# Products without a result on TensorE, ahead of and inside the first attention of an eight-block transformer kernel

## The chip, the cores and the metric

The kernel runs on one core of a Trainium2 chip. The metric is the device time of one execution in microseconds (us), as the median of several runs. Five engines with queues of their own matter here: TensorE (PE in the profile, with PEld for its weight loads), VectorE (DVE), ScalarE (ACT), GpSimd (POOL) and SyncE (SP, which issues the transfers). Each engine runs its instructions in order, and the engines wait for one another by semaphores.

## The reference, cut to what matters

The input x is 2 sequences of 512 tokens with 512 features. Eight blocks follow one another, each of the form x + f(layernorm(x)). The change lies in the first one, an attention with small latents:

```python
C_q  = x @ Wq_d + bq_d            # 512 -> 12
C_kv = x @ Wkv_d + bkv_d          # 512 -> 4
q = (C_q @ W_qk + b_qk).reshape(b, s, 32, 4)
scores = einsum('bqhd,bkd->bhqk', q, C_kv) / sqrt(4)
attn = softmax(scores, -1)
V = (C_kv @ Wv_u + bv_u).reshape(b, s, 32, 16)
out = einsum('bhqk,bkhd->bqhd', attn, V).reshape(b, s, 512)
return out @ Wo + bo
```

The seven blocks behind it (feed-forward with adapters, two larger attentions, a smaller one and two routed feed-forwards) are untouched.

## The kernel before

`attn0a_block` computes the first attention. It has two parts.

**The opening.** The 1024 tokens are 8 tiles of 128. For each tile t, VectorE takes the mean and variance (`norm.statistics`, L90 and L92) and forms factors (L100, L102), ScalarE takes the root (L96) and normalises the tile (`norm.normalise`, L109), TensorE turns it with four 128x128 transposes (`norm.turn`, L118), and ScalarE and VectorE copy the turned tile out of PSUM as a high and a low part (L123, L127). The tiles arrive by one DMA each. Between tiles 5, 6 and 7 TensorE starts on the latent projection (`latents`, three products for each block of 128 features, L37 to L39), and finishes it behind tile 7 in one stream: parts 0 to 3 of `latents`, with the first queries (`project_queries(0)`) between them.

**The steps.** 16 steps, each for 4 groups of heads and one sequence, run in a software pipeline over `step` and `g` (8 values of g in a step). In the step's own turn, `scores(step, g)` (L1584) writes scores by query into one of two PSUM tiles, and VectorE takes maxima over them (`maximum`, L1467). One call of `scores` is issued an iteration ahead: iteration g issues the scores of g + 1. When the maxima of a step are there, TensorE turns them (`turn_maxima`, L1569) and VectorE forms the shifted queries (`shift`, L1473, behind the first maximum of the next step in its queue). One step later TensorE computes the scores again by key (`scores_by_key`, L1596, two PSUM tiles `by_key`), ScalarE takes their exponentials (L1364), and TensorE multiplies by the values (`times_v`, L1618). In this stage, three bf16 products of zeros by the mask constant (`add_zeros`, L1608) add nothing to `out`; they stand in iterations 3, 5, 7 and 1 from step 1 on. Step 0 has only `scores`, `turn_values` (L1535) in its first two iterations, and `project_queries(1)` in iteration 1; on ScalarE it has nothing but the values' copy and one signed copy of queries.

`zeros` is a 128x128 bf16 tile that GpSimd fills at the start (L1312, semaphore `s_zeros`). `m.ident16` and `m.mask` are bf16 constants that arrive by DMA (semaphore `s_const`). Two later attentions have products of the same kind: eight of them at L2326 in `attn0b_block` and five at L3471 in `attn1b_block`, all of 256 columns of the mask constant by the bf16 identity.

Of the kernel before, what the change touches and what calls it, by code (L numbers as in the profile page):

```python
# [25 lines left out]
P = 128  # L26
# [1167 lines left out]
def attn0a_block(nc, m, d, prefix):  # L1194
# [19 lines left out]
    fills = [("Q", 0)]  # L1214
# [10 lines left out]
    with ExitStack() as ctx:  # L1225
# [24 lines left out]
        zeros, s_zeros = n.sb("zeros", [P, P], BF16), n.sem("zeros")  # L1250
        by_query = [n.ps(f"by_query{i}", [P, 2, SEQ]) for i in range(2)]
        by_key = [n.ps(f"by_key{i}", [P, SEQ]) for i in range(2)]
        aux, out = n.ps("aux", [P, QT, P]), n.ps("out", [P, QT, P])
# [16 lines left out]
        s_pv, s_osb, s_recip, s_out = [n.sem(k) for k in ("pv", "osb", "recip", "tokens")]  # L1270
        block = ctx.enter_context(nc.Block(no_gpsimd_drain=True))
        LOADS = 4
        aux_flat = aux[:, :, :].rearrange("p t q -> p (t q)")

        @block.sync
# [44 lines left out]
        def _(act):  # L1320
            act.wait_ge(s_eps, 1)
            norm.root(act, m, 0)
            for t in range(TILES + 1):
# [6 lines left out]
                if t == 3:  # L1330
                    act.wait_ge(s_load, 16 * LOADS)
                    act.activation(down_hi[:, :, :], down[:, :, :], ACT.Copy).then_inc(s_hi, 1)
# [186 lines left out]
        def _(pe):  # L1519
            def latents(g, parts=range(KT)):  # L1520
                pe.wait_ge(norm.s_lo, QT * (g // 2 + 1))
                if g >= 2:
                    pe.wait_ge(s_latev, g - 1)
                for k in parts:
                    last = mm3(pe, proj[g % 2], pair(down_hi, down_lo, slice(None), k, bass.ts(g % 2, P)),
                               pair(m.xnT_hi, m.xnT_lo, slice(None), k, bass.ts(g // 2, SEQ)),
                               start=k == 0, stop=k == KT - 1)
                    if k == KT - 1:
                        last.then_inc(s_lat, 1)

            def turn_values(b):

                pe.wait_ge(s_latev, 2 * (b + 1))
                for at in range(QT):
                    last = pe.transpose(out[:, b, bass.ts(at, VW)], lat[VROWS, 1, bass.ts(b * QT + at, P)],  # L1535
                                        m.ident[VROWS, VROWS])
                last.then_inc(s_vps, 1)

            def merge(k):

                last = pe.matmul(by_query[0][bass.ts(k, VW), 0, :], wv[:, k, :], wo[:, k, :], start=True, stop=True)
                if k == KT - 1:
                    last.then_inc(s_merged, 1)

            def merge_bias(k):
                if k == 0:
                    pe.wait_ge(s_wo, 48)
                last = pe.matmul(by_query[1][:, 0, :], bv[:, k, :], wo[:, k, :], start=k == 0, stop=k == KT - 1)
                if k == KT - 1:
                    last.then_inc(s_bias_v, 1)  # L1550
# [7 lines left out]
            def project_queries(step):  # L1558
                turn, b = divmod(step, BATCH)
                pe.wait_ge(s_lo, 3 + min(step, 1))  # L1560
                aux_free(("Q", step))
                mm3(pe, aux_flat, pair(wqk_hi, wqk_lo, slice(None), bass.ts(turn, P)),
                    pair(lat_hi, lat_lo, slice(0, QLAT + 1), bass.ts(b, SEQ)), start=True, stop=True).then_inc(s_aux, 1)

            def turn_maxima(step):
                pe.wait_ge(s_max, NG * (step + 1))
                aux_free(("M", step))
                for qt in range(QT):
                    last = pe.transpose(aux[:, qt, :], negmax[:, step % 2, qt, :], m.ident[:, :])  # L1569
                last.then_inc(s_aux, 1)  # L1570

            def scores(step, g):
                qt, a = g // 2, 1 - g % 2
                b = step % BATCH
                if NG * step + g >= 2:
                    pe.wait_ge(s_max, NG * step + g - 1)
                if g == 0:
                    pe.wait_ge(s_q, step + 1)
                    pe.wait_ge(s_kmix, 1 + min(step, 1))
                if step == 0 and g < 2:  # L1580
                    pe.wait_ge(s_latev, 3 + g)
                for e in range(2):
                    rows = slice(GROUP * (2 * a + e), GROUP * (2 * a + e + 1))
                    last = pe.matmul(by_query[g % 2][:, e, :], queries[rows, step % 2, bass.ts(qt, P)],  # L1584
                                     keys[rows, bass.ts(b, SEQ)], start=True, stop=True)
                last.then_inc(s_by_query, 1)

            def scores_by_key(step, u):
                kt, j = divmod(u, G)
                b = step % BATCH  # L1590
                if NU * step + u >= 2:
                    pe.wait_ge(s_exp, NU * step + u - 1)
                if u == 0:
                    pe.wait_ge(s_shifted, step + 1)
                rows = slice(GROUP * j, GROUP * (j + 1))
                pe.matmul(by_key[u % 2][:, :], keys[rows, bass.ts(b * QT + kt, P)], shifted[rows, step % 2, :],  # L1596
                          start=True, stop=True).then_inc(s_by_key, 1)
# [14 lines left out]
            def times_v(step, kt):  # L1612
                turn, b = divmod(step, BATCH)
                pe.wait_ge(s_exp, NU * step + G * (kt + 1))
                if kt == 0 and step >= 1:
                    pe.wait_ge(s_osb, step)
                for j in range(G):
                    last = pe.matmul(out[VW * j:VW * (j + 1), :, :].rearrange("v t q -> v (t q)"),  # L1618
                                     values[:, b * QT + kt, :],
                                     probsT[step % 2][:, kt, j, :, :].rearrange("p t q -> p (t q)"),  # L1620
                                     start=kt == 0, stop=kt == QT - 1)
                last.then_inc(s_pv, 1)

            def back_to_tokens(step):
                pe.wait_ge(s_osb, step + 1)
                aux_free(("T", step))
                for qt in range(QT):
                    last = pe.transpose(aux[:, qt, :], o_sb[:, step % 2, qt, :], m.ident[:, :])
                last.then_inc(s_aux, 1)

            pe.wait_ge(s_ident, 16)
            for t in range(TILES):
                norm.turn(pe, m, t)
                if t == 5:
                    pe.wait_ge(s_lo, 1)
                    latents(0, range(0, 1))
                if t == 6:
                    latents(0, range(1, 2))
# [3 lines left out]
            project_queries(0)  # L1642
            latents(3)
            pe.wait_ge(s_ones, 1)
            pe.wait_ge(s_zeros, 1)
            pe.wait_ge(s_const, 32)
            scores(0, 0)
            for step in range(STEPS + 2):
                for g in range(NG):
                    if g == 0 and step >= 2:  # L1650
                        scores_by_key(step - 2, NU - 2)
                        scores_by_key(step - 2, NU - 1)
                    if g >= 1 and 1 <= step <= STEPS:
                        scores_by_key(step - 1, 2 * g - 2)
                        scores_by_key(step - 1, 2 * g - 1)
                    after = NG * step + g + 1
                    if after < NG * STEPS:
                        scores(after // NG, after % NG)
                    if g == 0 and 1 <= step <= STEPS:
                        turn_maxima(step - 1)  # L1660
                    if g in (0, 2) and step >= 2:
                        times_v(step - 2, 2 + g // 2)
                    if g in (4, 6) and 1 <= step <= STEPS:
                        times_v(step - 1, (g - 4) // 2)
                    if g == 1 and step + 1 < STEPS:
                        project_queries(step + 1)
                    if step == 0 and g < BATCH:
                        turn_values(g)
                    if step == STEPS and 1 <= g <= 2:
                        merge_bias(2 * g - 2)  # L1670
                        merge_bias(2 * g - 1)
                    if step == STEPS and 3 <= g <= 4:
                        merge(2 * g - 6)
                        merge(2 * g - 5)
                    if g == 3 and 1 <= step <= STEPS:
                        add_zeros(first=step - 1)
                    if g in (5, 7) and 1 <= step <= STEPS or g == 1 and step >= 2:
                        add_zeros()
                    if g == 5 and step >= 2:
                        back_to_tokens(step - 2)  # L1680
# [2013 lines left out]
```

## Time and profile before

| | |
|---|---|
| median of 3 runs | 2195.97 us (2193.91 to 2198.79) |
| the profiled execution's own time | 2193.78 us |
| its span, first to last instruction | 2192.1 us |
| TensorE busy | 2046.3 us, 93% of the span |
| mean granted TensorE clock | 0.974 of full speed |

The durations in the next section come from the one profiled execution. The difference between its own time and its span, 1.68 us, lies around the first and last instruction. The granted clock of a stretch is 1.00 at the 2.4 GHz level and 0.50 at the 1.2 GHz level.

### The profile page before, as it was taken

What the parts mean: (1) busy time and instruction counts of PE and PEld (TensorE: products, weight loads), DVE (VectorE), ACT (ScalarE), POOL (GpSimd) and SP (SyncE); (2) the same over time, 40 slices, a digit from 0 to 9 for tenths busy, and PEclk for the clock granted to TensorE, in tenths of its full rate; (3) what the DMA queues carried; (4) which work ended last, traced back from release to release, by engine and by line L of the source; (5) the groups of instructions that cost most, each with busy time, mean ns of one, the idle gap of its engine ahead of it and who ended that gap; (6) DMA issues with size and microseconds to landing.
All of it is one profiled execution on the core that took longest, in us unless ns stands there. A gap on an engine that the chain in (4) does not pass through costs nothing. (4 is left out here: it accounts for less than half of the span.)

```text
span 2192.1 us, 33417 instructions
## 1 busy us (share of the span) xinstructions
PE 2046.3 (93%) x11617; PEld 1467.6 (67%) x11617; DVE 1391.3 (63%) x2509; ACT 1164.6 (53%) x2691; POOL 832.0 (38%) x1011
## 2 busy tenths in 40 slices
PE   6999988999999999999998789999999987999988
PEld 4333356777888888888876667777777765844457
DVE  6888574546666666666655646666666556777756
ACT  5777553245655656566554555555555534345553
POOL 0000100145545545455340145545554421747611
PEclk8999989999999999999999999999999999999999
DMA  3000022761112021121111344344333220744301
GB/s 121 1 1 1 3 97 81 222 197 39 48 40 67 22 68 39 49 68 39 30 39 51 93 111 114 91 105 116 91 92 73 61 73 30 215 89 73 73 25 39
DMA packets 95733, 158.10 MB, mean 72 GB/s; under 512 B 12064, under 2 KB 33568, under 8 KB 93391
## 3 DMA queue, kind: packets, MB, share of 16 engines
q1 hardware_dynamic: 85774, 134.19, 21.6%
q0 software_dynamic: 9792, 21.77, 4.2%
q8 instruction: 95, 1.56, 0.3%
q14 instruction: 72, 0.58, 0.1%
HBM read 90.91 MB, written 31.46 MB: 56 GB/s over the span
## 5 line engine op out<-in xcount | busy, mean ns | idle before, releaser
L2576 POOL TENSOR_TENSOR attn1a_probs<-attn1a_probs,attn1a_recip 128x128 f32<-128x128 f32 (+3 forms) x256 | 179.1, 721 | 231.8 <-DVE attn1a_recip L2759 231.2
L1917 POOL TENSOR_TENSOR attn0b_probs<-attn0b_probs,attn0b_recip 128x128 f32<-128x128 f32 (+3 forms) x256 | 196.6, 790 | 184.0 <-DVE attn0b_recip L2161 184.0
L2630 ACT ACTIVATE attn1a_probs<-attn1a_scores,attn1a_negmax 128x128 f32<-128x128 f32 (+3 forms) x256 | 132.9, 525 | 172.8 <-DVE attn1a_negmax L2745 171.6
L2021 ACT ACTIVATE attn0b_probs<-attn0b_scores,attn0b_negmax 128x128 f32<-128x128 f32 (+3 forms) x256 | 133.0, 525 | 121.4 <-DVE attn0b_negmax L2154 120.9
L1467 DVE TENSOR_REDUCE attn0a_negmax<-attn0a_by_query 128x2 f32<-128x1024 f32 x128 | 151.9, 1219 | 10.2 <-PE attn0a_by_query L1584 10.2
L2745 DVE TENSOR_REDUCE attn1a_negmax<-attn1a_scores 128x2 f32<-128x256 f32 (+3 forms) x128 | 105.4, 824 | 68.8 <-PE attn1a_scores L2950 68.8
L1910 POOL TENSOR_TENSOR attn0b_q_cos<-attn0b_q_cos,attn0b_q_swap 128x512 f32<-128x512 f32 x64 | 84.4, 1318 | 159.2 <-DVE attn0b_q_swap L2143 159.2
L2029 ACT ACTIVATE attn0b_probsT_hi<-attn0b_turned 128x256 fp32r<-128x256 f32 (+3 forms) x128 | 90.2, 704 | 87.4 <-PE attn0b_turned L2305 85.8
L2154 DVE TENSOR_REDUCE attn0b_negmax<-attn0b_scores 128x2 f32<-128x256 f32 (+3 forms) x128 | 105.0, 820 | 45.8 <-PE attn0b_scores L2294 45.8
L2962 PE MATMUL attn1a_turned<-ident_f,attn1a_probs 128*128 128x128 f32 x640 | 116.0, 279 | 8.8 <-DVE attn1a_probsT L2753 7.4
L2140 DVE TENSOR_TENSOR attn0b_q_cos<-attn0b_aux,attn0b_cos_q 128x512 f32<-128x512 f32 x60 | 41.5, 692 | 115.9 <-ACT attn0b_q_swap L2042 115.9
L2962 PEld LDWEIGHTS attn1a_turned<-ident_f,attn1a_probs 128*128 128x128 f32 x640 | 75.8, 141 | 50.6 <-POOL attn1a_probs L2576 19.8
L2166 DVE TENSOR_TENSOR attn0b_probsT_lo<-attn0b_turned,attn0b_probsT_hi 128x256 fp32r<-128x256 f32 (+3 forms) x128 | 104.4, 816 | 5.0 <-ACT attn0b_probsT_hi L2029 4.3
L1317 POOL TENSOR_TENSOR x_resident<-x_resident,attn0a_out_bias 128x512 f32<-128x512 f32 x8 | 9.9, 1281 | 256.3 <-DVE attn0a_out_bias L1489 256.3
L37 PE MATMUL attn0b_aux<-xnT,attn0b_wq_hi 128*128 128x512 f32 x240 | 99.6, 415 | 4.6 <-DVE x_resident L2176 2.4
L2305 PE MATMUL attn0b_turned<-ident_f,attn0b_probs 128*128 128x128 f32 x640 | 91.3, 273 | 10.4 <-DVE attn0b_probsT_lo L2166 10.4
L37 PE MATMUL attn0b_aux<-attn0b_wo_hi,attn0b_oT_hi 128*128 128x512 f32 x256 | 100.0, 391 | 0.9 <-DVE x_resident L2176 0.9
L2042 ACT ACTIVATE attn0b_q_swap<-attn0b_aux 64x512 f32<-64x512 f32 x120 | 71.2, 593 | 55.4 <-PE attn0b_aux L39 53.2
L39 PE MATMUL attn0b_aux<-attn0b_wo_lo,attn0b_oT_hi 128*128 128x512 f32 x256 | 100.1, 391 | 0.0
L38 PE MATMUL attn0b_aux<-attn0b_wo_hi,attn0b_oT_lo 128*128 128x512 f32 x256 | 99.6, 389 | 0.0
L2305 PEld LDWEIGHTS attn0b_turned<-ident_f,attn0b_probs 128*128 128x128 f32 x640 | 77.2, 141 | 29.0 <-DVE attn0b_probsT_lo L2166 12.7
L2946 PE MATMUL attn1a_scores<-xnT,attn1a_qT 128*128 128x128 f32 (+3 forms) x256 | 92.2, 360 | 3.3 <-DMA attn1a_qT<-attn1a_stage 3.3
(543 smaller groups left out, 6187.5 us busy)
## 6 DMA issues: line engine op xcount, KB each, us to landing
pre<-in_b_o SPq DMA_DIRECT2D x16, 1024.0 KB, 5.6
attn1a_qT<-attn1a_stage SPq DMA_DIRECT2D x128, 128.0 KB, 3.2
attn1a_qT<-attn1a_stage SPq DMA_DIRECT2D x64, 256.0 KB, 3.9
attn0b_vals<-attn0b_v_out SPq DMA_DIRECT2D x16, 512.0 KB, 3.7
attn0b_keys<-attn0b_part SPq DMA_DIRECT2D x32, 256.0 KB, 4.2
pre<-in_b_q SPq DMA_DIRECT2D x8, 1024.0 KB, 7.6
attn0b_kT<-attn0b_keys SPq DMA_DIRECT2D x64, 128.0 KB, 2.8
pre<-in_b_kv SPq DMA_DIRECT2D x5, 1024.0 KB, 6.8
```

The source lines that it names most:

```text
L37: pe.matmul(out, lhs[0], rhs[0], start=start, stop=False)
L39: return pe.matmul(out, lhs[0], rhs[1], start=False, stop=stop)
L1467: dve.tensor_reduce(into, by_query[g % 2][:, :, :], AX.X, ALU.max, negate=True).then_inc(s_max, 1)
L1917: pool.tensor_tensor(x, x, recip[:, r % DEEP, e:e + 1].broadcast_to([P, (qt + 1) * P]), ALU.mult).then_inc(s_scaled, 1)
L2021: act.activation(probs[:, r % DEEP, e, 0:width], scores[r % 2][:, e, 0:width], ACT.Exp, bias=negmax[:, r % 2, e:e + 1], accum_out=sums[:, ...
L2154: dve.tensor_reduce(negmax[:, r % 2, :], scores[r % 2][:, :, 0:(qt + 1) * P], AX.X, ALU.max, negate=True).then_inc(s_max, 1)
L2166: dve.tensor_tensor(of_pair(probsT_lo, at, qt, p), turned[:, :, 0:qt + 1, :], of_pair(probsT_hi, at, qt, p).bitcast(F32), ALU.subtract).th ...
L2305: last = pe.transpose(turned[:, e, k, :], probs[:, r % DEEP, e, bass.ts(k, P)], m.ident[:, :])
L2576: pool.tensor_tensor(x, x, recip[:, r % DEEP, e:e + 1].broadcast_to([P, (qt + 1) * P]), ALU.mult).then_inc(s_scaled, 1)
L2630: act.activation(probs[:, r % DEEP, e, 0:width], scores[r % 2][:, e, 0:width], ACT.Exp, bias=negmax[:, r % 2, e:e + 1], accum_out=sums[:, ...
L2745: dve.tensor_reduce(negmax[:, r % 2, :], scores[r % 2][:, :, 0:(qt + 1) * P], AX.X, ALU.max, negate=True).then_inc(s_max, 1)
L2962: last = pe.transpose(turned[:, k, :], probs[:, r % DEEP, e, bass.ts(k, P)], m.ident[:, :])
```

## The change

Three groups of products are added to TensorE's queue, none with a result that anything reads, and one wait moves.

- `WARM_START`: 48 products of zeros by zeros (128 columns each) ahead of the wait for the identity and the first tile. The wait for `s_zeros`, which stood ahead of the first scores, moves in front of them.
- `WARM`: 14 such products behind the transposes of each of tiles 0 to 4.
- `FILLS`: in step 0, in each iteration g from 1 to 7, five bf16 products of 256 columns of the mask constant by the bf16 identity, behind the scores. They write the first `by_key` tile, which nothing uses before step 1.

```diff
+        WARM_START, WARM, FILLS = 48, (14, 14, 14, 14, 14), 5
...
+            def warm_up(fills):
+
+                for _ in range(fills):
+                    pe.matmul(out[:, 0, :], zeros[:, :], zeros[:, :], start=True, stop=True)
+
+            pe.wait_ge(s_zeros, 1)
+            warm_up(WARM_START)
             pe.wait_ge(s_ident, 16)
             for t in range(TILES):
                 norm.turn(pe, m, t)
+                if t < len(WARM):
+                    warm_up(WARM[t])
                 if t == 5:
                     pe.wait_ge(s_lo, 1)
                     latents(0, range(0, 1))
...
             pe.wait_ge(s_ones, 1)
-            pe.wait_ge(s_zeros, 1)
             pe.wait_ge(s_const, 32)
             scores(0, 0)
...
                     if step == 0 and g < BATCH:
                         turn_values(g)
+                    if step == 0 and g >= 1:
+                        for _ in range(FILLS):
+                            pe.matmul(by_key[0][:, 0:2 * P], m.ident16[:, :],
+                                      m.mask[:, :, :].rearrange("p e x -> p (e x)"), start=True, stop=True)
```

## Rows read from the trace of the kernel before

**Rows 1.** Windows: length, busy PE, PEld, DVE, ACT, POOL; clock; DMA share, GB/s
```profile
39.35:47.37 8.02, 5.54 (x16) 2.17 (x16) 7.22 (x7) 0.23 (x1) 0.00 (x0) 0.50 0.52 195
47.37:56.20 8.83, 7.89 (x34) 3.43 (x34) 7.21 (x7) 4.81 (x9) 0.00 (x0) 0.50 0.00 1
61.89:75.40 13.51, 12.70 (x91) 5.15 (x95) 11.18 (x13) 9.65 (x19) 0.00 (x0) 1.00 0.00 1
1921.00:1927.00 6.00, 6.00 (x51) 3.92 (x49) 5.58 (x6) 0.00 (x0) 0.02 (x1) 1.00 1.42 198
1930.00:1933.80 3.80, 3.58 (x21) 1.75 (x20) 3.03 (x3) 2.97 (x7) 0.64 (x1) 0.99 0.00 0
1933.90:1937.00 3.10, 3.10 (x18) 1.13 (x16) 1.23 (x1) 0.69 (x2) 0.64 (x1) 0.50 0.00 0
```

**Rows 2.** Timeline of the opening: start, duration, instruction, idle before it and releaser
```profile
0.84 0.21 POOL L1312 MEMSET attn0a_zeros<- 128x128 bf16 x1
8.12 2.09 PE L118 MATMUL attn0a_by_query<-ident_f,attn0a_o_sb 128*128 128x128 f32 x8 [8.12 <-ACT attn0a_o_sb L109]
11.83 1.12 PE L118 MATMUL attn0a_by_query<-ident_f,attn0a_o_sb 128*128 128x128 f32 x4 [1.63 <-ACT attn0a_o_sb L109]
...
18.12 1.12 PE L118 MATMUL attn0a_by_query<-ident_f,attn0a_o_sb 128*128 128x128 f32 x4 [1.20 <-ACT attn0a_o_sb L109]
...
21.17 0.81 ACT L109 ACTIVATE attn0a_o_sb<-x_resident,attn0a_norm_offset,attn0a_norm_rstd 128x512 f32<-128x512 f32 x1 [0.69 <-DVE attn0a_norm_offset L102]
...
22.36 0.60 PE L118 MATMUL attn0a_by_query<-ident_f,attn0a_o_sb 128*128 128x128 f32 x4
```

**Rows 3.** Timeline of VectorE in steps 0 and 1
```profile
40.84 5.74 DVE L1467 TENSOR_REDUCE attn0a_negmax<-attn0a_by_query 128x2 f32<-128x1024 f32 x5
47.37 0.69 DVE L1473 TENSOR_TENSOR attn0a_shifted<-attn0a_aux,attn0a_queries 128x512 fp32r<-128x512 f32 x1 [0.80 <-PE attn0a_aux L1569]
50.95 1.23 DVE L1467 TENSOR_REDUCE attn0a_negmax<-attn0a_by_query 128x2 f32<-128x1024 f32 x1 [0.63 <-PE attn0a_by_query L1584]
...
56.62 1.23 DVE L1467 TENSOR_REDUCE attn0a_negmax<-attn0a_by_query 128x2 f32<-128x1024 f32 x1 [1.40 <-PE attn0a_by_query L1584]
58.25 1.23 DVE L1467 TENSOR_REDUCE attn0a_negmax<-attn0a_by_query 128x2 f32<-128x1024 f32 x1 [0.41 <-PE attn0a_by_query L1584]
59.70 1.23 DVE L1467 TENSOR_REDUCE attn0a_negmax<-attn0a_by_query 128x2 f32<-128x1024 f32 x1 [0.23 <-PE attn0a_by_query L1584]
61.89 0.69 DVE L1473 TENSOR_TENSOR attn0a_shifted<-attn0a_aux,attn0a_queries 128x512 fp32r<-128x512 f32 x1 [0.96 <-PE attn0a_aux L1569]
```

**Rows 4.** Timeline of TensorE in step 0 and the turn of its maxima
```profile
45.50 0.79 PE L1584 MATMUL attn0a_by_query<-attn0a_keys,attn0a_queries 32*128 32x512 f32 x2 [0.34 <-DVE attn0a_negmax L1467]
46.22 1.11 PE L1569 MATMUL attn0a_aux<-ident_f,attn0a_negmax 128*128 128x128 f32 x4
```

**Rows 5.** Timeline of like products elsewhere: eight, five and three in a row
```profile
52.29 0.82 PE L1608 MATMUL attn0a_out<-mask_bf,attn0a_zeros 128*128 128x256 bf16 x3
59.11 0.50 PE L1584 MATMUL attn0a_by_query<-attn0a_keys,attn0a_queries 32*128 32x512 f32 x2
59.54 0.50 PE L1608 MATMUL attn0a_out<-mask_bf,attn0a_zeros 128*128 128x256 bf16 x3
...
1103.72 0.28 PE L2294 MATMUL attn0b_scores<-mask_bf,ident_bf 128*128 128x128 bf16 x2
1103.84 1.04 PE L2326 MATMUL attn0b_aux<-mask_bf,ident_bf 128*128 128x256 bf16 x8
...
1921.13 0.71 PE L3471 MATMUL attn1b_out<-mask_bf,ident_bf 128*128 128x256 bf16 x5
1921.81 0.50 PE L3420 MATMUL by_query<-attn1b_k_mix,attn1b_q_mix 64*128 64x512 f32 x2
```

**Rows 6.** Instructions of line 1608: duration in ns, least, median, most
```profile
L1608 PEld LDWEIGHTS attn0a_out<-mask_bf,attn0a_zeros x192: 95/98/147, 52.3 to 267.7; 128*128 128x128 bf16 x192
L1608 PE MATMUL attn0a_out<-mask_bf,attn0a_zeros x192: 272/273/418, 52.3 to 267.8; 128*128 128x256 bf16 x192
```

## The prediction, made before the run

> **What bounds the kernel now.** I read the page's busy line first: TensorE is busy for 93% of the span and its mean granted clock is 0.974, so little of the 2192 us can come back through the clock at all. The rest is read in the stages that the change touches: the timeline of each engine from 0 to 76 us, and windows over it for the clock.
>
> The opening is not bound by TensorE. Tiles 0 and 1 are turned from 8.12 us on, and after that each group of four transposes starts as soon as ScalarE has normalised the tile; TensorE is idle for 1.63 us before tile 2 and 1.20 us before tile 5 [rows 2]. Its clock is low here: the window's column of granted clock shows 1.00, since no change of level is recorded yet, but four transposes take 1.12 us until tile 5 and 0.60 us at tile 7, so the clock rose to its 2.4 GHz level at about 22 us. From tile 7 on TensorE runs the latents in one stream, at the high level already, and that stream sets the time.
>
> Step 0 is bound by VectorE. From 40.84 us on one maximum follows another (1.13 us each: 5.74 us for five, less the last one's 1.22, over four) with the scores always there in time [rows 3]. TensorE has two small products for each maximum, and at 39.35 us its clock falls to the 1.2 GHz level, where it stays until 56.2 us, 16.85 us in all [rows 1]. While VectorE sets the pace this costs nothing; it costs where TensorE is waited for: at the turn of the maxima (VectorE idle for 0.80 us ahead of the shift at 47.37) and in step 1, where VectorE is idle for 0.63, 1.40, 0.41, 0.23 and 0.96 us [rows 3]. Step 1 takes 14.52 us from shift to shift (47.37 to 61.89), step 2, with more work in it, 13.51 us [rows 1, 3].
>
> **The change part by part.**
>
> WARM_START, 48 products. They can start when the zeros are there, at 0.84 + 0.21 = 1.05 us [rows 2]. Three products of 256 columns at the low clock take 0.82 us, the longest one 0.418, so they follow each other at (0.82 - 0.418) / 2 = 0.20 us [rows 5, 6]; with 128 columns I take half, 0.10 us. 48 take 4.8 us and end at 5.9 us, earlier if the clock rises under them; tile 0 is wanted at 8.12. The cover is 2.2 us, so the cost is 0. If a weight load did not hide behind so short a product, each would take 0.147 + 0.10 = 0.25 us [rows 6], the 48 would end at 13 us, and tile 0 would be 5 us late. Two such products of 128 columns in a row take 0.28 us, two of 128 columns and eight of 256 together (0.12 us between the starts of the groups) show one load and product in 0.06 us at the high clock [rows 5], so the loads do hide. The moved wait is met at 1.05 us and costs nothing where it stood or stands; behind it are the wait for the identity and everything else of TensorE.
>
> WARM, 14 products behind each of tiles 0 to 4. At the high clock 14 x 0.06 = 0.84 us, with the four transposes at 0.60 it makes 1.4 us, while tile 5 starts (18.12 - 11.83) / 3 = 2.1 us a tile behind tile 2 on average [rows 2]: hidden. Tile 1, which follows tile 0 at once before, starts at 8.12 + 1.4 = 9.5 and ends at 10.1 us, no later than the 10.21 us (8.12 + 2.09) at which the pair ends now [rows 2]. Cost 0. At the low clock it would be 1.05 + 1.4 = 2.5 us for each tile: tile 5 would be turned at 8.12 + 5 x 2.5 = 20.6 instead of 18.12 us, so up to 2.5 us are lost.
>
> What a high clock brings in the opening: ScalarE's last normalisation ends at 21.17 + 0.81 = 21.98 us and tile 7 starts at 22.36, since a group of latent products at the low clock stands before it [rows 2]. With them short, it starts at about 22.02: 0.34 us, and no more, because that normalisation waits for VectorE and not for TensorE. Bounds 0 and 0.34; I take 0.3.
>
> FILLS, 7 times five products. The nearest row is the later attention: the five there take 0.68 us from start to the next scores, at a cadence near 1.2 us, and the clock stays at 1.00 for all of the 6 us [rows 1, 5]. Here a pair of scores takes 0.43 us until the next product starts (59.11 to 59.54) [rows 5], and 0.43 + 0.68 = 1.11 us is just inside VectorE's 1.13 us. So the cover is thin: in the worst case 0.05 us is lost in each of seven iterations, 0.35 us; in the row of the later attention VectorE is busy for 5.58 of 6 us. I take 0.1 us as the cost, bounds 0 and 0.4.
>
> What a high clock brings in step 0 and at its end: nothing while the maxima run. Then the scores at 45.50 take 0.43 instead of 0.72 us until the transposes can start, and those 0.60 instead of 1.11 us [rows 2, 4]: the turned maxima are there at about 46.5 instead of 47.33 us. VectorE ends its queue of maxima at 40.84 + 5.74 = 46.58, so of its 0.80 us of idle time nearly all goes. I take 0.7 us, bounds 0 and 0.8.
>
> A rule of the Trainium skill speaks against that term. TensorE: Matmul & The Clock Gate, PE-mode transpose, says that the high clock does not engage for transposes and that one takes some 275 ns. The rows show four in 1.12 us before the clock rose and four in 0.60 us after, so here it does. By the page the term would be 0.3 us, and the sum 0.4 us smaller.
>
> Step 1. VectorE's work in it is 10.89 us (14.52 less the five waits of 3.63 us). At the high clock the last wait, 0.96 us, stays: step 1 already ran that part at the high level. The two that fell into the low stretch, 0.63 and 1.40 us, shrink to what step 2 shows in the same places (0.17 us each), which gives 1.7 us; the 0.41 and 0.23 us behind them may shrink too, as ScalarE is then ahead. The upper bound is 3.63 - 0.8 = 2.8 us. The lower bound is 0, since no fills stand in step 1: the clock may fall again. In the later attention it does, some 7 us after the last fills, although TensorE was busy for 3.58 of the 3.80 us before it fell, and it stays low for 3.1 us [rows 1]. A stretch like that would cost 3.1 of the 8.83 low microseconds here, a third of the gain, 0.6 us. I give it about even odds and take 1.4 us.
>
> The sum: 0.3 + 0.7 + 1.4 - 0.1 = 2.3 us less. Behind step 1 every step waits for the one before, so the gain moves the rest forward. The profiled execution would go from 2193.78 to 2191.5 us. Its time lies 2.2 us under the median of the three runs, so for the median I predict 2195.97 - 2.3 = 2193.7 us. A measurement of this kernel tells no change from one of under 0.2%, 4.4 us, and this is 0.1%. All four terms at their best give 0.34 + 0.8 + 2.8 = 3.9 us, still under it.
>
> **The rivals.**
>
> A. The clock holds through step 1 and that step comes down to VectorE's work: 3.9 us less, 2192.1 us, and a little luck of the runs makes it more than 0.2%. For it: ScalarE is busy for only 9.65 of the 13.51 us of step 2, and step 1 has less for TensorE. Against it: step 2 at the high clock still has 2.3 us without VectorE work [rows 1].
>
> B. The change doesn't do what it says in part: in step 1 the clock is lost at once, as soon as the fills end, and only the turn of the maxima and the opening gain: 0.3 + 0.7 - 0.1 = 0.9 us less, 2195.1 us.
>
> C. The products do not keep the clock up, and TensorE becomes the bound of step 0. This is the rival on the other side. It decides at one point: whether the clock is high when the fills run. At the low clock five fills take 1.0 to 1.1 us and a pair of scores 0.72, together 1.8 us against VectorE's 1.13. That is 0.7 us for each of the five iterations from 39.35 us on, 3.4 us, and in the opening up to 2.5 us; 5.9 us more in all, 2201.9 us. If the clock then rises under the dense stream, about half of it. Against it: in the later attention the same five products hold the clock, and so do the zeros of line 1608 through step 2 [rows 1, 5]. For it: those streams were at the high level when they began, and no row shows zeros by zeros.
>
> D. The weight loads don't hide behind 128 columns, and tile 0 is 5 us late: 2195.97 + 5 - 2 = 2199 us. The pair of such products above speaks against it. By the page's rule on transposes the time would be 2194.1 us instead of 2193.7; I leave it a chance of 2 in 100.
>
> **How the numbers follow.** The forecast gets 0.58, the page's case 0.02, A 0.15, B 0.15, C 0.07, D 0.03. Faster by over 0.2% is most of A's half that the runs' spread helps, and a tail of the forecast, since the three runs themselves spread over 4.9 us: 0.18. Slower by over 0.2% is C with half of its weight, part of D and the spread: 0.07. The rest, 0.75, is within 0.2%. The range for 8 in 10: down to 2190.5 us (A and 1.6 us of spread), up to 2198.0 us (B and the spread of the runs above their median, with C and D outside).
>
> **What would show each step right or wrong.** In the profile after: 48 products from about 1.1 us that end before 8 us, and four transposes of tile 0 or 1 in 0.6 us; tile 7 at 22.0; the granted clock at 1.00 from there to 47 us; the maxima of step 0 still 1.13 us apart; the shift of step 0 at about 46.3 us; the next shift 12.8 to 13.2 us later, at about 59.4 us instead of 61.89, and the rest of the timeline moved by that. The prediction is wrong if the maxima of step 0 stand further apart, if tile 0 is late, if the clock stays at 0.50 somewhere in step 0, or if the later blocks give the 2 us back.

## The result, and the profile after

The changed kernel takes 2201.48 us (median of 20 runs, 2193.47 to 2204.73); the kernel before took 2196.38 us in the same comparison (20 runs, 2193.12 to 2199.70). The medians lie 5.1 us apart; the ratio is 1.0018 with an interval of 1.0012 to 1.0025, some 4 us slower, where 2.3 us faster was forecast. The profiled execution took 2197.85 us, one of the shorter of the 20, and its span is 2195.1 us, 3.0 us more than before's. One run of the experiment e9_hold took 3231.17 us at a mean granted clock of 0.552; it is left out of all that follows.

The opening, from the timeline of TensorE in the changed kernel (start, duration, instruction, idle before it):

```profile
1.10 4.57 PE L1635 MATMUL attn0a_out<-attn0a_zeros 128*128 128x128 bf16 x48 [1.10 <-POOL attn0a_zeros L1313]
8.13 1.07 PE L118 MATMUL attn0a_by_query<-ident_f,attn0a_o_sb 128*128 128x128 f32 x4 [2.46 <-ACT attn0a_o_sb L109]
9.00 1.70 PE L1635 MATMUL attn0a_out<-attn0a_zeros 128*128 128x128 bf16 x14
10.49 1.06 PE L118 MATMUL attn0a_by_query<-ident_f,attn0a_o_sb 128*128 128x128 f32 x4
...
12.24 0.61 PE L118 MATMUL attn0a_by_query<-ident_f,attn0a_o_sb 128*128 128x128 f32 x4
12.68 0.94 PE L1635 MATMUL attn0a_out<-attn0a_zeros 128*128 128x128 bf16 x14
...
18.31 1.07 PE L118 MATMUL attn0a_by_query<-ident_f,attn0a_o_sb 128*128 128x128 f32 x4 [0.87 <-ACT attn0a_o_sb L109]
...
22.24 0.66 PE L118 MATMUL attn0a_by_query<-ident_f,attn0a_o_sb 128*128 128x128 f32 x4
```

The 48 products end at 5.67 us, in the cover forecast for them. The clock rises under them (their durations fall from 314 to 219 ns), is lost by tile 0 at 8.13 us (1.07 us for four transposes), is high again for tiles 2 to 4, and low again for tile 5 at 18.31. Tile 1 ends at 11.55 us, later than the 10.21 at which the pair ended before, but tile 2 isn't normalised before 11.97 us. Tile 7 starts at 22.24 us against 22.36 [rows 2]: 0.12 us.

The two profiles don't start alike, though. VectorE's statistics of tile 2 wait for the tile's transfer, and that came 0.19 us later in the changed kernel (before first, then the change):

```profile
9.78 0.69 DVE L90 BATCH_NORM_STATS2 attn0a_norm_stats<-x_resident 128x6 f32<-128x512 f32 x1 [1.60 <-DMA x_resident<-in_x]
```

```profile
9.97 0.69 DVE L90 BATCH_NORM_STATS2 attn0a_norm_stats<-x_resident 128x6 f32<-128x512 f32 x1 [1.77 <-DMA x_resident<-in_x]
```

From there to tile 7 the kernel before takes 12.58 us and the change 12.27, so the opening itself gained 0.31 us, and a later transfer hid most of it.

Step 0, from the same timeline, and two windows (length, busy time of PE, PEld, DVE, ACT, POOL, granted clock, DMA):

```profile
37.09 0.72 PE L1680 MATMUL attn0a_by_key<-mask_bf,ident_bf 128*128 128x256 bf16 x5
38.00 0.50 PE L1585 MATMUL attn0a_by_query<-attn0a_keys,attn0a_queries 32*128 32x512 f32 x2 [0.19 <-DVE attn0a_negmax L1468]
38.43 0.86 PE L1680 MATMUL attn0a_by_key<-mask_bf,ident_bf 128*128 128x256 bf16 x5
39.23 0.79 PE L1585 MATMUL attn0a_by_query<-attn0a_keys,attn0a_queries 32*128 32x512 f32 x2
39.95 1.25 PE L1680 MATMUL attn0a_by_key<-mask_bf,ident_bf 128*128 128x256 bf16 x5
41.13 0.79 PE L1585 MATMUL attn0a_by_query<-attn0a_keys,attn0a_queries 32*128 32x512 f32 x2
41.85 1.25 PE L1680 MATMUL attn0a_by_key<-mask_bf,ident_bf 128*128 128x256 bf16 x5
...
49.45 1.11 PE L1570 MATMUL attn0a_aux<-ident_f,attn0a_negmax 128*128 128x128 f32 x4
```

```profile
39.50:49.50 10.00, 10.00 (x38) 4.36 (x38) 7.37 (x7) 0.01 (x1) 0.00 (x0) 0.50 0.40 146
49.50:59.00 9.50, 8.53 (x40) 3.87 (x38) 7.21 (x7) 4.81 (x9) 0.00 (x0) 0.50 0.00 1
```

Only the first group of fills and most of the second run at the high level (0.72 us). The clock falls at 38.9 us, about where it fell before (39.35), and from then on the five products of a group take 1.25 us from the start of the first to the end of the last. An iteration is now 1.90 us long (39.95 to 41.85), 0.72 until the fills start and 1.18 until the next scores, and VectorE waits for the scores. TensorE is busy without a gap for 10 us, and the clock stays at 0.50; it comes back at 59.4 us.

VectorE's timeline in the same steps:

```profile
40.78 2.41 DVE L1468 TENSOR_REDUCE attn0a_negmax<-attn0a_by_query 128x2 f32<-128x1024 f32 x2
43.87 1.23 DVE L1468 TENSOR_REDUCE attn0a_negmax<-attn0a_by_query 128x2 f32<-128x1024 f32 x1 [0.68 <-PE attn0a_by_query L1585]
...
50.60 0.69 DVE L1474 TENSOR_TENSOR attn0a_shifted<-attn0a_aux,attn0a_queries 128x512 fp32r<-128x512 f32 x1 [1.71 <-PE attn0a_aux L1570]
...
65.02 0.69 DVE L1474 TENSOR_TENSOR attn0a_shifted<-attn0a_aux,attn0a_queries 128x512 fp32r<-128x512 f32 x1 [0.96 <-PE attn0a_aux L1570]
```

The five maxima that took 5.74 us in one piece [rows 3] now have gaps of 0.68 us, and the shift waits 1.71 us instead of 0.80. The first shift is 3.23 us late (50.60 against 47.37), the second 3.13 us (65.02 against 61.89), and the span is 3.0 us longer: the whole loss of this execution arises in step 0. Three iterations are 0.77 us longer than VectorE's 1.13 (the last maximum starts at 47.67 us against 45.36), and the turn of the maxima costs 0.9 us more: TensorE comes to it behind its last fills and scores, 0.55 us after VectorE's last maximum has ended (49.45 us against 48.90), where before it came 0.36 us ahead of that (46.22 against 46.58).

### The profile page after: what moved, and what is told of

The parts are those of the page before. It is cut to its first block and busy times, and to the rows that moved or that the text cites. A ratio compares the mean times of both kernels' runs of the same rounds, so it can differ in the third digit from the quotient of the medians.

```text
span 2195.1 us, 33722 instructions
## 1 busy us (share of the span) xinstructions
PE 2060.2 (94%) x11770; PEld 1479.3 (67%) x11770; DVE 1391.4 (63%) x2509; ACT 1164.5 (53%) x2691; POOL 832.0 (38%) x1011
```

## The experiments

The start of step 0 moves from one execution to another (the first maximum starts between 33.44 and 35.37 us in the profiles below), and so do the later blocks. So the stage is read by differences: from VectorE's statistics of tile 2, which wait for the tile's transfer, to the first maximum (opening), from the first maximum to the first shift (step 0), and from shift to shift (step 1). The statistics start between 9.08 and 10.60 us. All times are in us, each row's from one profiled execution. Each ratio is against runs of before on the same chip; e7_ten and e8_data_late were timed once, 2198.47 and 2204.79 us.

| kernel | opening's products | fills | ratio, interval | first maximum | opening | step 0 | step 1 | clock low in steps 0 and 1, from, to (us) |
|---|---|---|---|---|---|---|---|---|
| before | none | none | | 34.38 | 24.60 | 12.99 | 14.52 | 39.3, 56.4 |
| before again | none | none | 1.0003 (0.9993 to 1.0012) | 33.59 | 24.47 | 13.00 | 14.44 | 38.4, 55.4 |
| the change | yes | 5, from iteration 1 | 1.0018 (1.0012 to 1.0025) | 34.32 | 24.35 | 16.28 | 14.42 | 38.9, 59.4 |
| the change again | yes | 5, from iteration 1 | 1.0020 (1.0011 to 1.0029) | 34.47 | 24.36 | 16.29 | 14.40 | 39.0, 59.5 |
| e1_opening | yes | none | 1.0004 (0.9995 to 1.0012) | 34.66 | 24.37 | 12.99 | 14.52 | 36.7, 57.2 |
| e2_fills | none | 5, from iteration 1 | 1.0026 (1.0017 to 1.0036) | 35.37 | 25.33 | 17.57 | 14.35 | 37.7, 61.6 |
| e3_two | none | 2, from iteration 1 | 1.0004 (0.9995 to 1.0012) | 35.02 | 25.00 | 13.51 | 14.48 | 37.0, 57.4 |
| e7_ten | yes | 10, from iteration 1 | | 33.76 | 24.35 | 14.84 | 13.93 | 51.4, 58.2 |
| e8_data_late | yes | 2 of data, from iteration 1 | | 34.95 | 24.35 | 17.71 | 14.08 | 36.7, 60.6 |
| e5_earlier | yes | 5, from the first scores | 1.0003 (0.9994 to 1.0012) | 34.94 | 24.34 | 12.25 | 14.21 | 49.1, 55.9 |
| e6_data | yes | 2 of data, from the first scores | 1.0013 (1.0003 to 1.0023) | 34.58 | 24.35 | 12.25 | 15.39 | 50.3, 60.6 |
| e9_hold | yes | e5 and step 1 | 0.9999 (0.9990 to 1.0009) | 34.49 | 24.36 | 12.25 | 12.98 | never |
| e10_hold_alone | none | e5 and step 1 | 1.0003 (0.9993 to 1.0012) | 33.44 | 24.36 | 12.24 | 16.63 | 51.3, 65.0 |
| e11_hold_tiles | yes, and 6 behind tiles 5, 6 | e5 and step 1 | 0.9994 (0.9985 to 1.0003) | 34.05 | 24.35 | 12.25 | 12.98 | never |

**The parts alone.** Each edit is against the changed kernel.

```diff
-        WARM_START, WARM, FILLS = 48, (14, 14, 14, 14, 14), 5
+        WARM_START, WARM, FILLS = 48, (14, 14, 14, 14, 14), 0    # e1_opening
+        WARM_START, WARM, FILLS = 0, (), 5                       # e2_fills
+        WARM_START, WARM, FILLS = 0, (), 2                       # e3_two
```

> Only the 48 products at the start and the 14 behind each of tiles 0 to 4 stay; step 0 has no fills. Theory F (the fills of step 0, run at the low clock, are the whole loss): the time of before within 2 us (2194.5 to 2198.5), step 0's maxima 1.13 us apart, shift of step 0 at about 47.4 us. Theory O (the opening's products also cost, by a clock that falls or stays low later): 2 us or more above before, with a longer stretch of 0.50 in step 1 than before's 16.85 us in all.

> Only the fills of step 0 stay; the opening is as before. Theory F: all of the change's loss, 3 to 6 us above before (2199 to 2202), maxima 1.90 us apart where the clock is low. Theory O: clearly less than the whole change, 0 to 2 us above before.

> Only the fills, two in each iteration instead of five. Theory F, by the low clock's spacing: 0.72 us for the scores and 2 x 0.21 + 0.1 for the fills make 1.2 us, so an iteration costs at most 0.1 us more than VectorE's 1.13 us: within 1 us of before, if the clock falls at about 39 us as before. Theory H (fills hold the clock if there are enough of them): no difference from five in kind, since five don't hold it. A gain of 1 us or more would speak against both.

> The changed kernel unaltered, for a second profile: most of its 20 runs took 2201 to 2204 us, while the profiled one took 2197.85. Theory F: the profile of a typical run shows the same 1.90 us between maxima, and the further 4 us come from a longer stretch at the low clock in step 1 or from an earlier fall in step 0. Theory L: they come from a stage behind the first attention, and steps 0 and 1 look as in the first profile.

The opening alone changes the time by nothing that its interval could show (1.0004, 0.9995 to 1.0012). The table's column does show what it does: 24.34 to 24.37 us in all nine profiles with the products, and 24.36, 24.47, 24.60, 25.00 and 25.33 in the five without them, in the order in which the clock first rose there (20.6, 21.3, 22.2, 23.3 and 24.0 us). So the products gain 0 to 1.0 us, 0.25 against before's first profile. The fills alone lose at least as much as the whole change (2203.62 against 2197.08 us), and their profile shows why: the clock fell at 37.7 us, before the first group, so all seven ran at the low level and step 0 took 4.6 us more than before's. Two fills at the low clock take 0.54 us until the next scores; an iteration is 1.26 us where TensorE doesn't wait, the five maxima take 5.85 us instead of 5.74, VectorE waits 1.07 us for the turn instead of 0.80, step 0 is 0.5 us longer, and the time shows no loss. Theory F stands, theory O falls: the opening's products neither cost nor cause it.

The second profile of the change, a run of 2200.49 us, has the same steps 0 and 1 to 0.02 us. Of its further 3.4 us of span 3.3 arise behind the first attention: from the first product of the feed-forward (275.3 and 275.4 us) to the end the two profiles take 1919.8 and 1923.1 us. So the part L of the expectation holds for the spread, and F for the loss. The 3.3 us of step 0 explain most of the 4 to 5 us by which the change is slower; where the rest comes from is not shown.

**Why the clock wasn't held.** In the change TensorE has little to do from 34 to 37 us, between the latents and the first fills; this is the light stretch of the texts below. e5_earlier adds two groups of fills in it (`keep_up(n)` is the fill's product, n times), and e6_data does so with two products of data for each five of constants. e7_ten doubles the change's fills where they are (FILLS = 10), and e8_data_late puts e6_data's products there.

```diff
             scores(0, 0)
+            keep_up(FILLS)                  # e5_earlier, e6_data
...
-                    if step == 0 and g >= 1:
+                    if step == 0:           # e5_earlier, e6_data
+                        keep_up(FILLS)
...
+                    # keep_up's product in e6_data and e8_data_late, FILLS = 2
+                    pe.matmul(by_key[0][:, :], m.xnT_hi[:, 0, 0:P], m.xnT_hi[:, 0, 0:SEQ], start=True, stop=True)
```

> The change, with its five fills also behind the first scores and in iteration 0, so that they start at about 34.2 us, some 3 us earlier and ahead of every fall of the clock seen so far (36.7 to 39.3 us). Theory T (the fills came too late: the light stretch of 34 to 38 us had decided the fall): the clock stays at 1.00 through step 0, the maxima stay 1.13 us apart, the shift of step 0 comes at about 46.5 us, and the kernel is 1 to 3 us faster than before. Theory K (products of this kind and number do not hold the clock beside the small score products): it falls between 36 and 41 us all the same, and the kernel is 4 to 7 us slower than before.

> As e5_earlier, but each group of fills is two products of 512 columns of normalised data (128 rows of xnT by 512 columns of it) instead of five of 256 columns of constants; 0.47 us a group at the high clock instead of 0.55. Theory T: as e5_earlier, the clock holds, 1 to 3 us faster than before. Theory K: if the kind of operand is what matters, the clock holds here and not in e5_earlier; if the number of busy columns is, it falls in both, and with 0.85 + 0.72 us an iteration at the low clock this one is 2 to 4 us slower than before.

> The change with ten fills instead of five in iterations 1 to 7. At the low clock an iteration takes 2 x 1.1 + 0.72 = 2.9 us. Theory T: the clock still falls between 37 and 40 us, decided by the light stretch before; with so dense a stream it then rises again within step 0, some 4 us later, and the iterations behind that take 1.5 to 1.6 us. Theory K in its strong form (a stream of such constants never raises the clock): low to the end of step 0, maxima 2.9 us apart, about 6 us more than the change.

> The change, its fills where they are (iterations 1 to 7), but of data: two products of 512 columns. Theory T: the clock falls between 36.7 and 39.5 us as in all kernels so far, and an iteration at the low clock takes 0.72 + 0.85 = 1.6 us, about 2 us more than before in step 0. Theory K (the operands matter): it doesn't fall, or rises again within step 0, although the change's constants did neither in 20 us.

The light stretch, in the change first, then in e5_earlier: TensorE is busy for 2.23 of 3.00 us, then for all of them.

```profile
34.00:37.00 3.00, 2.23 (x17) 1.22 (x15) 2.68 (x4) 1.75 (x3) 0.00 (x0) 1.00 0.01 3
```

```profile
34.00:37.00 3.00, 3.00 (x26) 1.82 (x25) 2.06 (x3) 1.93 (x3) 0.00 (x0) 1.00 0.04 8
```

In e5_earlier the clock is high through step 0; TensorE's and then VectorE's timeline, and the windows:

```profile
34.33 0.50 PE L1585 MATMUL attn0a_by_query<-attn0a_keys,attn0a_queries 32*128 32x512 f32 x2
34.76 0.72 PE L1639 MATMUL attn0a_by_key<-mask_bf,ident_bf 128*128 128x256 bf16 x5
35.41 0.50 PE L1585 MATMUL attn0a_by_query<-attn0a_keys,attn0a_queries 32*128 32x512 f32 x2
...
44.92 0.50 PE L1585 MATMUL attn0a_by_query<-attn0a_keys,attn0a_queries 32*128 32x512 f32 x2
45.36 0.72 PE L1639 MATMUL attn0a_by_key<-mask_bf,ident_bf 128*128 128x256 bf16 x5
46.06 0.50 PE L1585 MATMUL attn0a_by_query<-attn0a_keys,attn0a_queries 32*128 32x512 f32 x2
46.49 0.66 PE L1570 MATMUL attn0a_aux<-ident_f,attn0a_negmax 128*128 128x128 f32 x4
```

```profile
41.40 5.74 DVE L1468 TENSOR_REDUCE attn0a_negmax<-attn0a_by_query 128x2 f32<-128x1024 f32 x5
47.19 0.69 DVE L1474 TENSOR_TENSOR attn0a_shifted<-attn0a_aux,attn0a_queries 128x512 fp32r<-128x512 f32 x1
```

```profile
34.00:49.00 15.00, 13.40 (x89) 7.37 (x87) 14.01 (x15) 4.71 (x8) 0.00 (x0) 1.00 0.40 141
49.20:55.80 6.60, 6.41 (x27) 2.18 (x27) 5.19 (x5) 4.07 (x8) 0.00 (x0) 0.50 0.00 1
```

The same five products that made an iteration 0.77 us longer in the change cost nothing here: five maxima in 5.74 us, as before, and the shift follows them without a wait. Step 0 is 0.74 us shorter than before's. e6_data does the same with data (12.25 us), and e8_data_late with data from iteration 1 loses 4.7 us in step 0, as e2_fills does (clock down at 36.7 us, 1.87 us an iteration), so the operands' kind does not decide; theory K falls. In e7_ten, from iteration 1 like the change, the clock did not fall before 51.4 us, against what both theories said. Each of its groups takes 1.2 us until the next scores even at the high level, so step 0 is 1.85 us longer than before's all the same:

```profile
38.15 1.26 PE L1680 MATMUL attn0a_by_key<-mask_bf,ident_bf 128*128 128x256 bf16 x10
```

Theory T holds by count. Of the five kernels profiled with fills from the first scores on (e5, e6, e9, e10, e11), all kept the clock through step 0; of the six profiles with fills from iteration 1 on (the change twice, e2, e3, e7, e8), five lost it between 36.7 and 39.0 us. That fills in the light stretch keep the clock is shown by this; that a later start always loses it is not, by e7_ten. Whether its ten products or the chance of one execution kept the clock there, and whether ten would raise a clock that had fallen, stays open.

**Step 1.** In e5_earlier the clock falls at 49.1 us, and step 1 gains only 0.31 us. e9_hold adds products where TensorE waits for the shift and behind it; e10_hold_alone is e9_hold without the opening's products, and e11_hold_tiles is e9_hold with some more behind tiles 5 and 6. The cut shows what e9_hold adds to e5_earlier.

```diff
                     if g == 0 and 1 <= step <= STEPS:
                         turn_maxima(step - 1)
+                    if step == 1 and g == 0:
+                        pe.wait_ge(s_v, 1)
+                        keep_up_out(9)      # into out[:, 0:2, :]
...
+                    if step == 1 and g in (1, 2):
+                        keep_up_out(3)
```

> e5_earlier, and in step 1 nine more products of constants behind the turned maxima (TensorE waits there for the shift, about 1.3 us) and three in each of iterations 1 and 2, into the tile out before its first sum. Theory S (step 1 gained only 0.3 us in e5_earlier since the clock fell at 49.1 us, behind the light stretch of 46.5 to 49 us): the clock stays at 1.00 through step 1, the two shifts lie 12.5 to 13.2 us apart instead of 14.52, and the kernel is 2 to 3 us faster than before at the same state of the later blocks. Rival: TensorE's own work bounds step 1 and the shifts stay about 14 us apart even at the high clock.

> e9_hold without the products of zeros in the opening. If those gain something (the clock rises at 22 us in one profile of before and some 1 us later in two kernels with the same opening), this is 0.3 to 1 us slower than e9_hold, with the first maximum at 34.4 to 35.4 us. If they don't, the two are equal.

> e9_hold with six products of zeros also behind tiles 5 and 6. If the clock can be held through the opening, the transposes of tiles 5 to 7 all take 0.6 us and tile 7 starts 0.6 us behind the end of the pair before it; the time gains at most 0.3 us over e9_hold, since ScalarE and VectorE set the pace there. Rival: they delay the first latent products and cost 0.3 us or more.

Windows and VectorE's shifts of e9_hold:

```profile
34.00:47.00 13.00, 12.17 (x85) 7.06 (x86) 12.46 (x13) 4.16 (x6) 0.00 (x0) 1.00 0.48 163
47.00:60.00 13.00, 12.26 (x81) 5.13 (x82) 10.90 (x11) 9.16 (x17) 0.00 (x0) 1.00 0.01 2
```

```profile
46.74 0.69 DVE L1474 TENSOR_TENSOR attn0a_shifted<-attn0a_aux,attn0a_queries 128x512 fp32r<-128x512 f32 x1
...
59.72 0.69 DVE L1474 TENSOR_TENSOR attn0a_shifted<-attn0a_aux,attn0a_queries 128x512 fp32r<-128x512 f32 x1 [0.96 <-PE attn0a_aux L1570]
```

The clock never falls in the attention's first steps; step 0 takes 12.25 and step 1 12.98 us instead of 12.99 and 14.52, 2.28 us less together, and the next block starts at 270.0 instead of 272.1 us. Theory S holds for this profile. Yet the median, 2197.67 us, is that of before (2197.49), and the ratio's interval, 0.9990 to 1.0009, leaves room for a gain of 2.2 us at most. In its profile the rest from 270 us on takes 1924.6 us against before's 1920.0. Followed instruction by instruction, VectorE's queue is 2.2 us ahead of before's at 200 us and 1.1 at 1100, level with it from 1300 to 2090 us, and 2.2 us behind from 2120 us on. About half of the 4.6 us thus lies in the last block, in one window of both kernels (before first, then e9_hold):

```profile
2090.00:2190.00 100.00, 87.35 (x494) 66.58 (x491) 57.54 (x174) 40.61 (x77) 14.75 (x15) 0.96 0.10 35
```

```profile
2090.00:2190.00 100.00, 89.66 (x493) 67.48 (x490) 57.12 (x174) 40.50 (x76) 14.77 (x15) 0.93 0.08 27
```

The granted clock is lower there, in code that neither kernel changed. e10_hold_alone has no step 0 trouble either, but its clock fell at 51.3 us in spite of the products of step 1, and stayed low for 13.7 us: step 1 took 16.63 us. The same products are thus no guarantee, and the busy time does not tell the two apart (from 46.0 to 51.3 us TensorE is busy for 5.05 us here and for 5.17 in e9_hold). Its runs spread from 2195.37 to 2202.05 us; four of the eleven, the profiled one among them, took over 2201 us. The opening takes 24.36 us in both, so its products gained e9_hold nothing over this execution. e11_hold_tiles (2197.03 us) is the fastest of the family, and its ratio (0.9985 to 1.0003) lies below the change's, but its interval includes 1: no kernel here is shown to beat before. e6_data is slower than before by 0.13%, clear of its interval.

**Before again.**

> The kernel before, unaltered, for a second profile of it. From the first products of the feed-forward behind the first attention to the end, the profiles so far took 1919.8 to 1926.5 us, and those of the faster first attention (e9_hold, e11_hold_tiles) lie in the upper half of that. Theory V (the later blocks vary by themselves, by where the clock falls in them, and before's first profile caught a short case): this profile shows 1921 us or more there, or its other runs do by their spans. Theory G (an earlier arrival makes the later blocks longer): it shows 1920 us again. From the first maximum to the second shift it takes 27.5 us in both, if the clock falls at 36.7 to 39.3 us.

Steps 0 and 1 repeat (27.44 us together, 27.51 in the first profile). From the next block to the end this profile takes 1920.0 us again, which is what theory G said of it. But the spans of its other runs reach 2197.7 us with the same code, while the first maximum moves by only 2 us between all profiles, so the later blocks of before most likely vary by several microseconds too. Late arrivals have long cases as well (e2_fills 1924.9 us from 277.5 us on, e10_hold_alone 1926.5 from 273.8 on). Of the fourteen profiles, three of the four that reach the next block before 272 us take 1923 us or more from there, and five of the ten others; so few can't say whether an earlier arrival makes the long cases more frequent.

## Why the prediction was wrong

**The step that failed** is the one on FILLS: that the nearest row was the later attention, where five such products hold the clock, so that they would run at the high level, inside VectorE's 1.13 us. That row was of a stretch that came from dense work almost without a gap (TensorE busy for 5.86 of the 6 us before it). Here a light stretch, from 34 to 37 us, stands between the latents and the first fills, and the clock fell at 38.9 and 39.0 us in the two profiles of the change and at 37.7 in e2_fills. What the runs showed in place of the row's claim is an iteration of 1.90 us instead of 1.13, and a step 0 that is 3.29 us longer instead of 0.6 shorter. e5_earlier, which adds two groups in that stretch and changes nothing else, shows the row's claim come true: no cost, 12.25 us. So five products an iteration are enough where the clock is high when they begin.

**Rival C happened in step 0**, with a chance of 0.07 that was far too low, and at the point named for it: whether the clock is high when the fills run. Its price for step 0 was 3.4 us (0.7 us in each of five iterations). Measured were 3.29 us more in step 0 of the change, 1.90 us an iteration against 1.8 forecast, and 4.6 us in e2_fills, where all groups ran low. That 3.4 and 3.29 agree is in part luck: it was three iterations of 0.77 us and 0.9 us at the turn of the maxima, a term that C did not have. Its clause that a dense stream would bring the clock back failed: 20.5 us low, with TensorE busy throughout the first ten. Its 2.5 us for the opening did not come, so that its total, 2201.9 us, lies beside the measured 2201.48 is luck too.

**The opening**: 48 products hidden, right (5.67 us against 5.9); the gain of 0.3 us, right once the transfer of tile 2 is taken out. By the clock of the profile tile 7 gained 0.12 us and the first maximum 0.06, but the transfer came 0.19 us later; from it, tile 7 gained 0.31 us and the first maximum 0.25. Tile 1 was not ready at 10.1 us as forecast but at 11.55, since the clock was low from 8.2 us on; that cost nothing. The forecast took one execution for the kernel: over all profiles the transfer of tile 2 lets its statistics start between 9.08 and 10.60 us, and without the opening's products the clock rises between 20.6 and 24.0 us.

**The turn of the maxima**: 0.7 us at the high clock, right. It never came in the change; in e5_earlier it is 0.74 us. The Trainium skill (TensorE: Matmul & The Clock Gate, PE-mode transpose) says that the high clock does not engage for transposes, by which the term would be 0.3 us. That does not hold in these traces: four take 0.66 us at 46.49 us in e5_earlier and 1.11 us at 49.45 in the change.

**Step 1**: 1.4 us with even odds of a fall, 1.7 without. In the change it is 0.10 us, since the low stretch reached on to 59.4 us. Held in e9_hold it is 1.54 us; with a fall in it 0.31 us (e5_earlier) or a loss (e6_data, 0.87 us longer than before's). The size for a held clock was right, the price of a fall too low.

**The size of what is measured.** Held throughout, steps 0 and 1 gain 2.28 us in e9_hold, and with the opening 2.5. The terms of the prediction for a held clock make 2.6 (0.3 + 0.7 + 1.7 - 0.1), so their sizes were good, though it took products that the change does not have; that the sum's 2.3, with its odds of a fall in it, equals 2.28 is chance. The time shows neither.

## What to carry to other kernels

Products without a result are not free where the engine behind them sits close to TensorE's pace: cost them at the low clock too, 1.90 us an iteration here against 1.13, and ask what the clock is when the first one runs. Here they did better inside the light stretch than behind it (the clock kept through step 0 in five profiles of five against one of six). Two an iteration nearly fit at the low clock (0.5 us lost in step 0 and no gain); five lost 3 to 5 us there where they stood, and gained 0.7 us where they held the clock. And before two profiles are subtracted, look for what arrives from outside: here a transfer that moved by 1.5 us between executions hid what the opening gained.

## What the runs showed of the hardware

A busy TensorE did not get its clock back: from 39.5 to 49.5 us it was busy for 10.00 of 10.00 us at 0.50 in the change, with fills of constants, and in e8_data_late, with data; in e10_hold_alone it was busy for 13.50 of 13.50 us from 51.4 us on, at 0.50, in the work of step 1 itself. Nor did the clock need a long gap to fall: in the kernel before no idle time of TensorE from 34 us to the fall at 39.3 is longer than 0.83 us. The 48 products of zeros in the opening did raise it: they take 314 ns each at first and 219 ns at the end, with the change at about 4.7 us. In the change, as in the kernel before, it came back in step 1, at 59.4 and 56.4 us, 2.3 and 2.5 us behind the start of the first group of products by the values. In the other profiles that distance is 1.5 to 3.7 us, but 7.9 in e6_data and 12.9 in e10_hold_alone, so that group alone does not explain it. What in the work of TensorE makes the difference between these streams, the runs leave open.

The spread of a kernel that changes nothing is of the size of such a gain: the runs of before reach from 2192.86 to 2199.78 us, in part by where the clock falls in blocks much later.
